# Expert results sent to their tokens' places tile by tile, with the places riding in the rows, instead of gathers by token

## The reference

```python
def conv(x):                       # K=7, 16 groups of 8 channels
    r = relu((x @ w_reduce - mean) * (gamma / sqrt(var + eps)) + beta)   # 32 channels
    kgen = (r @ w_span + b_span).reshape(B, H, W, 16, 49)
    patches = ...                  # the 49 shifted copies of x
    return einsum('bhwgk,bhwkgc->bhwgc', kgen, patches)

def ffn(x):                        # N = 12544 tokens, D=128, H=256, E=8
    probs = softmax(x @ gate_w + gate_b)
    cw = the two largest probabilities of a token, zero for the other experts
    for e in range(8):
        out += cw[:, e, None] * (gelu(x @ W1[e] + b1[e]) @ W2[e] + b2[e])
    return out

x = x + conv(layernorm(x))
t = x.reshape(4, 3136, 128)
return (t + ffn(layernorm(t))).reshape(x.shape)
```

## Time and profile before

| | us |
|---|---|
| median of 3 runs | 1273.44 |
| lowest and highest | 1263.01, 1277.46 |
| the profiled execution | 1264.97 |
| its span, first to last instruction | 1263.0 |
| mean granted TensorE clock, share of full | 0.855 |
| busy: TensorE, VectorE, ScalarE, GpSimd | 946.3, 554.3, 526.4, 493.2 |

### The profile page before, as it was taken

One profiled execution on the slowest core, in us unless ns is written; L12 is line 12 of the kernel. 1 busy time (PEld: TensorE's weight loads), 2 busy tenths in 40 slices (PEclk: granted clock), 3 DMA queues, 4 the chain that ended last, 5 costly groups with the idle time before them and its releaser, 6 DMA issues. The chain is left out here.

```text
span 1263.0 us, 30108 instructions
## 1 busy us (share of the span) xinstructions
PE 946.3 (75%) x11249; PEld 815.6 (65%) x11249; DVE 554.3 (44%) x1722; ACT 526.4 (42%) x1246; POOL 493.2 (39%) x538
## 2 busy tenths in 40 slices
PE   1229989859988889988888889878889778526620
PEld 0127767758877778777777778767778667525520
DVE  4112344324454565446564463535654364404322
ACT  3214444334744546444654437444544235212310
POOL 4000010720146730756127650566307560667035
PEclk9999887678989979989899888987999895956975
DMA  5587562625436573636636474442725232223212
GB/s 118 110 188 204 115 146 48 164 54 136 103 86 178 126 167 82 166 90 155 154 75 173 120 166 94 125 127 72 168 67 148 74 85 60 67 73 90 78 45 65
DMA packets 184136, 144.05 MB, mean 114 GB/s; under 512 B 65166, under 2 KB 169614, under 8 KB 183544
## 3 DMA queue, kind: packets, MB, share of 16 engines
q1 hardware_dynamic: 169080, 116.41, 37.9%
q0 software_dynamic: 14336, 25.72, 7.9%
q10 hardware_dynamic: 576, 0.00, 0.0%
HBM read 89.70 MB, written 52.36 MB: 112 GB/s over the span
## 5 line engine op out<-in xcount | busy, mean ns | idle before, releaser
L1078 PE MATMUL kg<-rT,wk 98*112 98x112 f32 x1792 | 311.5, 318 | 33.2 <-DVE kb L764 26.8
L528 POOL DMA_INDIRECT xrows<-tn,pos x224 | 217.1, 969 | 303.7 <-DVE pos L894 173.3
L617 ACT ACTIVATE kb<-kg 112x448 f32<-112x448 f32 x336 | 181.4, 543 | 300.7 <-PE kg L1078 297.3
L1078 PEld LDWEIGHTS kg<-rT,wk 98*112 98x112 f32 x1792 | 247.0, 204 | 88.0 <-issue 47.0
L543 POOL DMA_INDIRECT got<-yrows,pos x224 | 214.0, 955 | 164.5 <-issue 68.4
L1113 PE MATMUL e<-kb,win 112*32 112x64 f32 x6272 | 219.4, 290 | 9.9 <-ACT kb L617 9.1
L659 ACT ACTIVATE hT<-h,staged 128x128 f32<-128x128 f32 x420 | 131.2, 364 | 172.8 <-PE h L1180 172.1
L1113 PEld LDWEIGHTS e<-kb,win 112*32 112x32 f32 x6272 | 160.1, 127 | 45.3 <-issue 17.9
L1192 PE MATMUL xy<-staged,hT 128*128 128x128 f32 x840 | 148.8, 316 | 53.4 <-ACT hT L659 30.6
L912 DVE COPY staged<-table 128x642 f32 x245 | 124.4, 508 | 102.6 <-DVE yo L921 55.8
L1180 PE MATMUL h<-xT,staged 128*128 128x128 f32 x840 | 153.5, 312 | 16.2 <-DVE staged L912 12.3
(11 more groups left out here) (105 smaller groups left out, 785.6 us busy)
## 6 DMA issues: line engine op xcount, KB each, us to landing
win<-xpad SPq DMA_DIRECT2D x56, 784.0 KB
xin<-xrows SPq DMA_DIRECT2D x56, 256.0 KB
yrows<-yo SPq DMA_DIRECT2D x56, 256.0 KB
xpad<-xs SPq DMA_DIRECT2D x280, 28.0 KB
xs<-in_x_dram SPq DMA_DIRECT2D x56, 112.0 KB
t_row<-in_x_dram SPq DMA_DIRECT2D x56, 112.0 KB
out_dram<-t_row SPq DMA_DIRECT2D x56, 112.0 KB
xrows<-tn SPq DMA_DIRECT2D x4, 896.0 KB, 8.3
```

Of the source, the lines that this page charges most:

```text
L528: pool.indirect_dma_start(xrows[n % 2], bass.IndirectOffsetOnAxis(ap=pos[n % 2][:, i:i + 1], axis=0), tn[:, c * C:(c + 1) * C], None) \
L617: act.activation(kb[:, lo:lo + 4 * PATCHES], kg_bank[j % 2][0:WIN, 0:4 * PATCHES], ACT.Copy) \
L1078: mm = pe.matmul(kg_bank[j % 2][0:WIN, i * PATCHES:(i + 1) * PATCHES], wk[:, at:at + WIN], r[:, :, :, b4 + i], start=True, stop=True, skip ...
```

## The change

**The place rides with the row.** Rows of `tn`, `xrows` and `xin` become 129 values long. GpSimd writes into the last value of each row the number of the place that the row's result is to have in a new DRAM tensor `yback`, which is laid out by token and choice (four small copies in a band, `scatter`). Rows that no token fills need a place too: at the start `mark_rows` writes the number of a spare row into the last value of all 8,960 rows of `xrows`, by two transfers of single values, once the zeroing has landed. VectorE takes the places of four tiles out of `xin` as integers (`take_place`).

**Results are scattered, not gathered.** For each tile GpSimd issues one indirect transfer of its 128 rows from `yo` to `yback` (`send_back`), as soon as the tile's bias is added and in the beat of that step. The stores to `yrows` and the 32 gathers are gone. SyncE loads a band's results in eight plain transfers of 112 by 512 values (`load_back`, beats 48 to 55, two buffers, each of the later six behind a mix), and VectorE adds them four columns at a time (beats 50 to 57), with the same 32 instructions.

**Beats.** Scatters take beats 10 to 45 instead of 10 to 31, and experts start in beat 47 instead of 33.

**The last band** leaves the beats. Its tiles run in loops of their own behind everything else of each engine: on SyncE its rows are loaded behind the store of band 5. It has three banks for the first product, two for the second, two for the turned rows, four buffers for staged experts and three for gelu's output; TensorE issues the first product two tiles ahead of the second; its results come back into eight separate places.

The core of the diff (renamed indices and the helpers that only choose a buffer are left out):

```diff
-    START = 33
-    SCATTER = (10, 32)
-    GATHER = (36, 54)
+    START = 47
+    SCATTER = (10, 46)
+    LOAD_BACK = START + 1
+    MIX = START + 3
+    CR1 = C + 1
...
-        xrows = [nc.dram_tensor(f"xrows{i}", [XROWS, C], F32, kind="Internal").ap() for i in range(2)]
-        yrows = [nc.dram_tensor(f"yrows{i}", [XROWS, C], F32, kind="Internal").ap() for i in range(2)]
...
+        xrows = [nc.dram_tensor(f"xrows{i}", [XROWS, CR1], F32, kind="Internal").ap() for i in range(2)]
+        BACK = 2 * T * COLS
+        yback = nc.dram_tensor("yback", [NC * BACK + 2 * XROWS, C], F32, kind="Internal").ap()
...
+        CONST = 16 + 2 * E
         zeros = tn
+        own_rows = got[:, 0:2 * (XROWS // T)]
         wk_raw = kb[0:KR, 0:G * K * K]
         wk_hi = kb[0:KR, G * K * K:2 * G * K * K]
 
         def by_col(tile):
             return tile[:, :].rearrange("p (k e) -> p k e", e=E)
 
-        def h_at(n, m):
-
-            return kg_bank[m % 2] if n == NC - 1 else h_bank
-
-        def y_at(n, m):
-            return e_bank[m % 2] if n == NC - 1 else xy_bank
+        def in_tail(n):
...
+            return n == NC - 1
+
...
             def store_out(n):
-                sp.wait_ge(mixed, 2 * COLS * (n + 1))
-                for a in range(2):
-                    for s in range(STRIPS):
+                for s in range(STRIPS):
+                    sp.wait_ge(mixed, 8 * n + 2 * s + 2)
+                    for a in range(2):
                         sp.dma_start(out[:, 8 * n + 2 * s + a, :, :].rearrange("b w c -> w b c"),
                                      cols(t_row[n % 3], 4 * s, 4)[a * W:(a + 1) * W]).then_inc(out_stored[n % 3], 16)
 
             def load_rows(n, g):
                 k = GROUPS * n + g
                 if g == 0:
-                    sp.wait_ge(scattered, 16 * 2 * COLS * (n + 1))
+                    for i in range(4):
+                        sp.wait_ge(scattered[i], 16 * 8 * (n + 1))
                 if k >= 2:
                     sp.wait_ge(xt_tiles, k - 1)
+                    sp.wait_ge(place_ready, k - 1)
...
+            def load_back(n, piece):
+
+                if piece == 0:
+                    sp.wait_ge(y_sent[0], sent(last_group(n, 0)))
+                    sp.wait_ge(y_sent[1], sent(last_group(n, 1)))
+                if not in_tail(n) and 8 * n + piece >= 2:
+                    sp.wait_ge(mixed, 8 * n + piece - 1)
+                if in_tail(n):
+                    sp.wait_ge(main_done, STEPS * NC)
+                    sp.wait_ge(mixed, 8 * n)
+                s, k = divmod(piece, 2)
+                rows = yback[n * BACK + k * T * COLS:n * BACK + (k + 1) * T * COLS, :]
+                sp.dma_start(got_at(n, piece), rows.rearrange("(p q) c -> p (q c)", p=T)[:, 4 * s * C:4 * (s + 1) * C]) \
+                    .then_inc(got_sem(n, piece), 16)
 
...
+            def mark_rows():
+                sp.wait_ge(rows_zero, 16 * 6)
+                with nc.allow_non_contiguous_dma(reason="8960 places, once"):
+                    for i in range(2):
+                        sp.dma_start(xrows[i].rearrange("(p k) c -> p k c", p=T)[:, :, C],
+                                     own_rows[:, i * (XROWS // T):(i + 1) * (XROWS // T)]).then_inc(rows_marked, 16)
...
 
             for beat in range(BEATS * (NC + 2)):
                 n, o = divmod(beat, BEATS)
                         load_x(2 * n + 5)
                     if o in (50, 52, 54) and n + 1 < NC:
                         load_window(n + 1, 0, (o - 48) // 2)
-                if o == START - 1 and 0 <= n - 1 < NC:
+                if o == START - 1 and 0 <= n - 1 < NC - 1:
                     load_rows(n - 1, 0)
                     load_rows(n - 1, 1)
                 for m, i, half in expert_parts(beat):
-                    if half == 0:
-                        continue
-                    if i % 4 == 0 and i // 4 + 2 < GROUPS:
+                    if half and i % 4 == 1 and i // 4 + 2 < GROUPS:
                         load_rows(m, i // 4 + 2)
-                    if i % 4 == 0 and i:
-                        store_rows(m, i // 4 - 1)
-                    if i == SLOTS - 1:
-                        store_rows(m, GROUPS - 1)
-                if o == 59 and 0 <= n - 2 < NC:
-                    store_out(n - 2)
+                if 0 <= n - 2 < NC - 1:
+                    if LOAD_BACK <= o < LOAD_BACK + 8:
+                        load_back(n - 2, o - LOAD_BACK)
+                    if o == MIX + 8:
+                        store_out(n - 2)
                 if o == 60 and n + 1 < NC:
                     load_t(n + 1)
+            for g in range(GROUPS):
+                load_rows(NC - 1, g)
+            for piece in range(8):
+                load_back(NC - 1, piece)
+            store_out(NC - 1)
...
+                for i in range(4):
+                    if sent_rows[i]:
+                        pool.wait_ge(scattered[i], sent_rows[i])
+                for i in range(2):
+                    if sent_y[i]:
+                        pool.wait_ge(y_sent[i], sent_y[i])
 
...
             def scatter(n, i):
+
                 if i == 0:
                     pool.wait_ge(pos_ready, n + 1)
                     if n < 2:
-                        pool.wait_ge(rows_zero, 16 * 6)
+                        pool.wait_ge(rows_marked, 16 * 2)
                 k, c = divmod(i, COLS)
+                q = i // 8
+                if i % 8 == 0:
+                    hf = q % 2
+                    if q >= 2:
+                        pool.wait_ge(scattered[q - 2], 16 * 8 * (n + 1))
+                    else:
+                        pool.wait_ge(tn_ready, 4 * n + 2 * hf + 2)
+                    pool.tensor_copy(tn[:, :].rearrange("p (c e) -> p c e", e=CR1)[:, 8 * hf:8 * hf + 8, C],
+                                     place_f[:, k * COLS + 8 * hf:k * COLS + 8 * hf + 8]).then_inc(placed, 1)
+                    marked["count"] += 1
+                    pool.wait_ge(placed, marked["count"])
                 pool.indirect_dma_start(xrows[n % 2], bass.IndirectOffsetOnAxis(ap=pos[n % 2][:, i:i + 1], axis=0),
-                                        tn[:, c * C:(c + 1) * C], None) \
-                    .then_inc(scattered, 16)
-                count["scattered"] += 16
-
-            def gather(n, i):
-                c, k = divmod(i, 2)
-                if i == 0:
-                    total = GROUPS * (n + 1)
-                    pool.wait_ge(y_stored[0], 16 * ((total + 1) // 2))
-                    pool.wait_ge(y_stored[1], 16 * (total // 2))
-                slot = i % 8
-                use = 2 * COLS * n + i
-                if use >= 8:
-                    pool.wait_ge(mixed, use - 8 + 1)
-                pool.indirect_dma_start(got[:, slot * C:(slot + 1) * C], None, yrows[n % 2],
-                                        bass.IndirectOffsetOnAxis(ap=pos[n % 2][:, k * COLS + c:k * COLS + c + 1], axis=0)) \
-                    .then_inc(got_row[slot], 16)
-                got_count[slot] += 16
+                                        tn[:, c * CR1:(c + 1) * CR1], None).then_inc(scattered[q], 16)
+                sent_rows[q] += 16
+
+            def send_back(n, i):
+
+                g = GROUPS * n + i // 4
+                if i == 0 and n >= 2:
+                    pool.wait_ge(mixed, 8 * (n - 1))
+                pool.wait_ge(y_out, NT * n + i + 1)
+                pool.indirect_dma_start(yback, bass.IndirectOffsetOnAxis(ap=place[g % 3][:, i % 4:i % 4 + 1], axis=0),
+                                        yo[g % 2][:, (i % 4) * C:(i % 4 + 1) * C], None).then_inc(y_sent[g % 2], 16)
+                sent_y[g % 2] += 16
...
+                    for i in rows_sent(o):
                         scatter(n - 1, i)
-                if 0 <= n - 2 < NC:
-                    for i in rows_moved(o, GATHER):
-                        gather(n - 2, i)
+                for m, i, half in expert_parts(beat):
+                    if half == 0:
+                        for k in tiles_out(i):
+                            send_back(m, k)
...
+            for i in range(NT):
+                send_back(NC - 1, i)
...
+
+            def take_place(n, g):
+
+                k = GROUPS * n + g
+                have = min(4, NT - 4 * g)
+                dve.wait_ge(xin_loaded[k % 2], 16 * (k // 2 + 1))
+                if k >= 3:
+                    dve.wait_ge(y_sent[(k - 3) % 2], sent(k - 3))
+                dve.tensor_copy(place[k % 3][:, 0:have],
+                                xin[k % 2][:, 0:have * CR1].rearrange("p (i e) -> p i e", e=CR1)[:, :, C]) \
+                    .then_inc(place_ready, 1)
 
             def put_y(n, i):
                 m = NT * n + i
                 g = GROUPS * n + i // 4
-                dve.wait_ge(y_done, m + 2 if i % 4 == 2 and i + 1 < NT and n < NC - 1 else m + 1)
-                if i % 4 == 0 and g >= 2:
-                    dve.wait_ge(y_stored[g % 2], 16 * (g // 2))
+                if i % 4 == 0:
```

(29 more changed lines are left out.)

186 lines of the change are left out of this document (120 added, 66 removed).

## The result

| | before | after |
|---|---|---|
| median, us | 1270.01 | 1331.43 |
| lowest to highest | 1263.01 to 1277.46 | 1323.99 to 1333.64 |
| span of the profiled execution | 1263.0 | 1331.9 |
| mean granted clock | 0.855 | 0.824 |

The changed kernel takes 1.0442 of the time (95% interval 1.0391 to 1.0494): it is 4.4% slower, where 1.4% faster was forecast, and 1331 is outside of the range.

What follows compares the result with a forecast made beforehand. Up to the convolution's end TensorE and its waits, mostly for scattered rows, were taken as the bound. +1 + 8 - 22 - 6 + 5 - 3 = -17 us took 1273.4 to 1256, range 1220 to 1290.

Steps and rivals of the forecast that it cites:

- the fifth term: Bands 2 to 6: GpSimd waiting for landed sends in front of the norms' powers costs +5 us (0 to 58).
- the cover that was named: At the norms' powers: TensorE has two banks of kernels ahead, an argument against landings being exposed; no size of its own.
- GpSimd's landings: Slower rival: every band's four powers meet sends not yet landed, 58 us if all exposed; 1292 at 70%; chance 0.2.
- a sign of being wrong: Norms' powers: the forecast would be wrong if ScalarE's wait for the power grew past 20 us.
- Band 1: forecast -22: Band 1 goes from 137.1 to 115 us with experts from beat 47: -22 (-15 to -27).
- no sends are among them: Band 1: its scatters get 14 beats more without sends between them, so no wait for `xin`.
- Bands 2 to 6: forecast -6: Bands 2 to 6: TensorE waits 14 us for rows instead of 16.8 and begins cold less often: -6 (-20 to +10).
- so the last ends at 24 + 66 + 2 + 3.6: Bands 2 to 6: GpSimd's last scatter ends 95.6 us into the band, or at 92 without `rstd1`.
- The marks: forecast +8 (0 to 13): Band 0: marks on SyncE shift later loads by 19 us, partly covered, and delay VectorE and TensorE: +8 (0 to 13).
- 1.64 ns a value: Marks in band 0: issue price from two earlier loads, making 14.7 us for 8,960 values; 10 was taken.
- The end: forecast -3: From the last band's first scatter on: 180.1 us, nearly all of the gathers' 50 us given back: -3 (-20 to +12).
- The start: Before the first norm: three index ramps on GpSimd cost +1 us.

Runs made afterwards that it cites:

- mended: Changed kernel without the wait for landed transfers ahead of both powers, and with the marks issued in beat 56 of band 0: 1286.97 us, ratio 1.0115.
- The kernel with early scatters: The mended kernel with scatters from beat 10 ending before beat 40 and the experts' start left at beat 47: 1281.58 us, ratio 1.0028.

## Why the prediction was wrong, step by step

**The landings: the right mechanism at a seventh of its price.** The step is the fifth term, "I take 1 us a band: +5", from "0.93 and 1.5 (the last gather took 2.43 from issue to landing)". It measured 34 us. The 1.5 is a landing in the last 50 us, where nothing else moves. At a band's end the same landing stands beside windows of 784 KB, loads back and the band's stores, and the waits for it took 2.8 to 7.1 us in band 3; the row with that price was at hand, the longest of GpSimd's waits for its gathers, 8.1 us. And the cover that was named, "TensorE has two banks of kernels ahead", didn't hold: of ScalarE's 53.7 us TensorE waited 45.8. The rival "GpSimd's landings" had the place, the chain and its size of 58 us; the measured 34 are 59% of it. It gave 1292 for 70% because it kept the other terms at -22. The prediction had also named this as a sign of being wrong, ScalarE's wait for the power past 20 us; it was 53.7.

**Band 1: forecast -22, measured -0.6** (mended, 130.0 and 132.8 where before took 137.1 to 140.6, so -4 to -11). The step "no sends are among them", so no wait for `xin`, looked at GpSimd only. The last scatter began at 278.62, and its rows were asked for at 286.56, as SyncE's own order put 28 stores of normed rows in front:

```profile
271.33 13.26 SPq L376 DMA_DIRECT2D xpad<-xs  x28
284.69 1.70 SPq L363 DMA_DIRECT2D xs<-in_x_dram  x4
286.56 5.40 SPq L421 DMA_DIRECT2D xin<-xrows  x3
```

TensorE waited 7.3 us for them, and then 8.4 for `tn` through the landings. The second half of the band took 82.8 us, as before; less band 0's 49.4 and these two waits, 17.7 are left for its nine tiles, 2.0 us apiece where 1.2 were assumed. The band's clock was 0.75; what made a tile that dear was not tested. The prediction counted what beat 47 was moved past on GpSimd, and not on SyncE.

**Bands 2 to 6: forecast -6.** In the mended kernel, where most of the landings are out (TensorE still waits 10.7 us for `tn`), bands 2 to 5 take 628 us against 586 to 594. The wait for rows came nearly as worked out in bands 2 to 4 (4 us forecast; 5.1, 4.6 and 5.1), and not in bands 5 and 6 (1 forecast; 4.9 and 7.9). The step behind it, "so the last ends at 24 + 66 + 2 + 3.6", added up GpSimd's own times as if it never waited on its way; it waits up to 3.8 us for a tile's bias with five scatters behind, also in band 5, which has no power in beat 32. In the changed kernel the waits of bands 2 to 6 are 25.7 us together, where 14 were forecast and 16.8 stood before. That is 12 of the term's error. The rest is larger, and the runs give it only in part: in band 4 the mended kernel has 4.2 us more of busy TensorE and 6.0 more of idle than the kernel before, and 6.3 of the sum stand in beats 40 to 56. The kernel with early scatters, which has no wait for rows in its bands 2 to 5, loses as much in bands 2 to 4 (478 us, mended 476, before 439 to 446), in band 4 mostly in front of the power of beat 32, and nothing in band 5. So the step that failed is the whole account of GpSimd in a band: up to beat 47 it has 20 sends more, and where they stand in front of rows or of a power, TensorE pays. How the rest divides between the waits and the clock stays open. The upper end of the term's range, +10, was also passed.

**The marks: forecast +8 (0 to 13).** Band 0 got 13.2 longer, and marks moved away gave 7.7 of it back. The parts came out otherwise, so that 13.2 lies at the end of the range and not far beyond it is in part luck: the issue took 4.2 us and not 10, and the load of x was put off by 10.4 us (130.05 before) and not 19. What was not in the sum is the landing. From 112 to 126 us, while the marks land, the DMA engines are fully busy (a share of 1.24) and move 10 GB/s, and a window of 784 KB was issued behind them; VectorE's moments began 11.8 us after the load of x was issued, and 8.6 before.

```profile
112.28 4.16 SPq L464 DMA_DIRECT2D xrows<-got  x2
...
140.47 2.15 SPq L363 DMA_DIRECT2D xs<-in_x_dram  x4
```

```profile
xrows<-got SPq DMA_DIRECT2D x2, 17.5 KB, 13.5
```

The two transfers of marks, 17.5 KB each, took 10.5 and 16.5 us from issue to landing. The Trainium skill's fit for DMAs issued from GpSimd (DMA: Bandwidth & Descriptors, Anatomy of one DMA) gives 2.04 us for such a size, as an estimate from that page. The marks were issued from SyncE and don't follow it; the measurement decides. The prediction was right not to go by it, though its own row of issue times, 1.64 ns a value, was 3.5 times too dear here (4.2 us for 8,960).

**The end: forecast -3, measured -12.4** from the first scatter on (183.2 before, 170.8 after). The 53 transfers took 68.2 (69.3 forecast), the way to the last band's first turned rows 25.5 (28.3). The 35 tiles took 57.4 (62): the granted clock was 0.50 only for the first 4 us behind the idle stretch (1253.7 to 1258) and 1.00 from 1260 on, where six tiles at half clock had been assumed, and a tile took 1.6 us behind VectorE (1.65). The rest took 19.6 (20.5). The parts are all right within 5 us, and each is below its forecast. Of the gathers' 50 us three quarters are given back, not nearly all.

**The start** cost 0.1 us, not 1. The sum is off by 86 us (+69 for -17, in the two profiled executions): 29 for the landings, 13 in band 1 besides its 8.4 of landings, 5 for the marks, less 9 at the end and 1 at the start, which leaves 49 for bands 2 to 6. The mended kernel, where most of the landings are out, has 34 to 42 more than the executions of before in bands 2 to 5 for the forecast's 6 less, which is 40 to 48 from the other side.

## What to carry over

A wait for "all that was issued has landed" is priced by the landing beside the largest transfer that can be in flight there, and never by one from the kernel's quiet end; find the longest case in the view of waits. When a step is moved to another beat, list what each queue has in front of it there, SyncE's too, and what each engine waits for on its way: GpSimd's requests alone gave the last scatter's end too early, since a send among them waits for its tile. An engine that is busy for 71% of a stretch with requests, as here in beats 24 to 40 (0.96 us each and 0.30 between two), is full for whatever is queued behind them: scatters placed earlier moved most of the delay to the next power.
